# Row maxima sent by GpSimd's queue, another order of query and key parts, and an earlier residual product, in a pipelined attention graph

## The reference, cut to what matters

```python
nodes = {-1: inputs}
for c in range(6):
    nsrc = min(c + 1, 5); snode = c - nsrc
    q = ew[c, 0] * (nodes[c - 1] @ We[eq] + be[eq])
    k = ew[c, 1] * (nodes[snode] @ We[ek] + be[ek])
    v = ew[c, 2] * (nodes[snode + nsrc // 2] @ We[ev] + be[ev])
    o = _mha(q, k, v, Wq[c], Wk[c], Wv[c], Wo[c])    # softmax over 256 keys, per batch and head
    nodes[c] = act_w[c] * o + q
out = layernorm(nodes[5]) * ln_g + ln_b
x = x + out
```

## Time and profile before

| | |
|---|---|
| Median of 3 runs | 1074.8 us (1071.63 to 1077.8) |
| Profiled execution, its own time | 1070.5 us |
| Its span, first to last instruction | 1068.3 us |
| Granted TensorE clock, mean | 0.984 |
| Busy: TensorE, VectorE, ACT, POOL | 991.6, 834.6, 732.0, 450.0 us |
| DMA issues: st (SP), mst (SP), stores (POOL) | 576 of 128 KB, 192 of 6 KB, 15 of 128 KB |

### The profile page before, as it was taken

The page is one execution under the profiler, slowest core; times in us unless marked ns, Lnnn a source line. Parts: engine busy times, 40 slices in busy tenths (PEclk is TensorE's granted clock), DMA queues, the critical chain, the costliest instruction groups (busy, mean ns, idle before and its releaser), DMA issues.

```text
span 1068.3 us, 26897 instructions
## 1 busy us (share of the span) xinstructions
PE 991.6 (93%) x9705; PEld 701.8 (66%) x9705; DVE 834.6 (78%) x1791; ACT 732.0 (69%) x1605; POOL 450.0 (42%) x885
## 2 busy tenths in 40 slices
PE   8889999988899999999999999999999999999994
PEld 4755656554676677677676777676776777767763
DVE  5557777766789987888788899878887887888883
ACT  3446666663677777777777777877777777777774
POOL 3522222332343334334543458743344335434455
PEclk9989999999999999999999999999999999999997
DMA  8100000006666666666567577666766766775640
GB/s 226 35 1 1 1 0 0 0 2 88 91 94 100 101 100 94 105 102 99 99 101 103 93 103 122 115 98 105 102 96 102 101 102 94 105 102 95 101 64 30
DMA packets 84439, 87.33 MB, mean 82 GB/s; under 512 B 11610, under 2 KB 70238, under 8 KB 84318
## 3 DMA queue, kind: packets, MB, share of 16 engines
q1 hardware_dynamic: 82670, 83.56, 50.6%
q0 software_dynamic: 848, 2.11, 1.0%
q10 hardware_dynamic: 800, 0.05, 0.0%
HBM read 6.90 MB, written 2.10 MB: 8 GB/s over the span
## 4 chain that ended last, share of the span: by engine, by line
PE 45%; DMA 17%; DVE 11%; SPq 10%; ACT 6%; issue 6%; POOL 5%; DVEq 0%; ACTq 0%; POOLq 0%
PE bank L1221 44%; DMA mst<-mrows 17%; SPq L494 7%; DVE region L1136 3%; SPq L508 2%; POOL hl L582 2%; ACT region L807 2%; POOL hl L579 1%; DVE region L1068 1%; DVE region L952 1%; DVE region L1063 1%; PE bank L1557 1%; ACT region L783 1%; DVE region L1056 1%; DVE region L1017 0%
## 5 line engine op out<-in xcount | busy, mean ns | idle before, releaser
L1136 DVE TENSOR_REDUCE region<-bank 128x2 f32<-128x512 f32 x768 | 488.5, 679 | 123.9 <-PE bank L1221 117.8
L807 ACT ACTIVATE region<-bank 128x512 f32<-128x512 f32 x768 | 409.7, 610 | 59.2 <-PE bank L1221 59.1
L1221 PE MATMUL bank<-st 48*128 48x256 f32 x3072 | 325.2, 330 | 5.6 <-DVE region L1136 4.2
L1221 PEld LDWEIGHTS bank<-st 48*128 48x128 f32 x3072 | 250.8, 189 | 28.2 <-DVE region L1136 4.7
L579 POOL TENSOR_TENSOR hl<-qk,one_col 128x512 fp32r<-128x512 f32 x96 | 99.9, 1041 | 400.0 <-ACT qk L772 400.0
L1221 PE MATMUL bank<-region 128*32 128x256 f32 (+3 forms) x3554 | 247.9, 375 | 2.2 <-DVE region L1163 1.2
L1221 PEld LDWEIGHTS bank<-region 128*32 128x32 f32 (+2 forms) x3554 | 129.2, 116 | 85.0 <-issue 16.4
L1221 PE MATMUL bank<-mst,ones 64*128 64x512 bf16 x768 | 151.3, 387 | 26.1 <-DMA mst<-mrows 23.6
L582 POOL TENSOR_TENSOR hl<-qk,hl 128x512 fp32r<-128x512 f32 x96 | 122.5, 1276 | 7.5
L829 ACT ACTIVATE mrows<-bank 24x256 bf16<-24x256 bf16 x96 | 35.8, 372 | 126.7 <-PE bank L1557 126.7
L1221 PEld LDWEIGHTS bank<-mst,ones 64*128 64x128 bf16 x768 | 37.2, 93 | 90.1 <-DMA mst<-mrows 39.1
(11 more groups left out here) (190 smaller groups left out, 1273.6 us busy)
## 6 DMA issues: line engine op xcount, KB each, us to landing
st<-hl SPq DMA_DIRECT2D x576, 128.0 KB, 4.4
mst<-mrows SPq DMA_DIRECT2D x192, 6.0 KB
out<-xall POOLq DMA_DIRECT2D x15, 128.0 KB, 3.8
xall<-in_L_attn_hidden_states SPq DMA_DIRECT2D x1, 768.0 KB, 9.2
cst<-in_constants SPq DMA_DIRECT2D x1, 514.5 KB, 4.1
xT<-in_L_ffn_Wq SPq DMA_DIRECT2D x1, 384.0 KB
xT<-in_L_ffn_Wk SPq DMA_DIRECT2D x1, 384.0 KB
xT<-in_L_ffn_Wv SPq DMA_DIRECT2D x1, 384.0 KB
```

The source lines that it names most:

```text
L807: act.activation(to, x_bank(x, k, e)[:, :].rearrange("p (j q) -> p j q", j=2), ACT.Exp).then_inc(B["exp_ok"], 1)
L1136: dve.tensor_reduce(mx[s.n % 2][:, to:to + 2], s_bank(s, k, e)[:, :].rearrange("p (j k) -> p j k", j=2), AX_X, ALU.max, negate=True).then_ ...
L1221: return pe.matmul(o, w, x, start=start, stop=stop, skip_group_check=skip)
```

## The change

There are three edits.

1. `maxima_rows` becomes a function of the engine that issues it. POOL calls it behind `split_maxima(m)` and ahead of everything else of its stage. SP keeps it in the stages in which POOL has work for last nodes (`by_sync`). Each of the two buffers of mst has a semaphore for either queue.
2. The four parts lie in hl in the order K_HI, Q_LO, K_LO, Q_HI. The two splits write them there with other steps.
3. `project` is cut in two. `residual(d)` issues the residual product between `project_qk` and the third burst; `project(d)` keeps the output projection.

```diff
-K_HI, K_LO, Q_HI, Q_LO = range(4)
+K_HI, Q_LO, K_LO, Q_HI = range(4)
...
-        m_in = [sem(f"m_in{n}") for n in range(2)]
+        m_in = [[sem(f"m_in{n}{q}") for n in range(2)] for q in ("_pool", "_sync")]
...
+        def by_sync(n):
+
+            ends = [at_slot(n + M_AT, k) for k in (W_AT, V_AT)]
+            return any(e is not None and e.last for e in ends)
+
+        def rows_in(m):
+
+            same = [n for n in range(m.n % 2, m.n + 1, 2) if by_sync(n) == by_sync(m.n)]
+            return m_in[by_sync(m.n)][m.n % 2], 32 * len(same)
+
+        def maxima_rows(eng, m):
...
+            eng.wait_ge(B["mt_ok"], m.n + 1)
+            for s in range(2):
+                of = s * MROW * JH
+                eng.dma_start(mst[m.n % 2][HALF * s:HALF * s + MROW, :, :], mrows[m.n % 2][of:of + MROW * JH, :]).then_inc(rows_in(m)[0], 16)
...
             def phase(t, a, s, m, x, d, z, w, v):
-                if m is not None:
-                    maxima_rows(m)
+                if m is not None and by_sync(m.n):
+                    maxima_rows(sp, m)
                 if a is not None:
                     stack(a)
...
-                pool.tensor_tensor(to[:, 1::2, :], qk[a.n % 2], to[:, 0::2, :].bitcast(F32), ALU.subtract)\
+                pool.tensor_tensor(to[:, K_LO:Q_LO - 1:-1, :], qk[a.n % 2], to[:, K_HI::Q_HI - K_HI, :].bitcast(F32), ALU.subtract)\
                     .then_inc(B["lo_ok"], 1)
...
                 if m is not None:
                     split_maxima(m)
+                if m is not None and not by_sync(m.n):
+                    maxima_rows(pool, m)
...
                 if k == 0:
-                    pe.wait_ge(m_in[x.n % 2], 32 * x.uses(2))
+                    pe.wait_ge(*rows_in(x))
...
-            def project(d):
+            def residual(d):
+
                 to, prev = bank[OUT], source(d, GRAPH[d.c]["src"][0])
                 pe.wait_ge(B["outT_ok"].sem, B["outT_ok"].at(d.n))
                 if not d.last:
                     mm(to[:, T:2 * T], w_res[:, d.c, :], prev, stop=False)
-                    pe.wait_ge(B["ctxT_ok"].sem, B["ctxT_ok"].at(d.n))
...
                     project_qk(a)
+                if d is not None:
+                    residual(d)
                 burst((3,), (3,))
```

More of the change, by code:

```diff
@@ L451, in final_scale @@
             eng.tensor_tensor(tiles, fyn, tiles, ALU.add).then_inc(B["out_ok"], 1)
+        def by_sync(n):
[5 more added lines that the diff above has]
+        def maxima_rows(eng, m):
+            old = at_slot(m.n, 2)
+            if old is not None:
+                eng.wait_ge(B["x_ps"], old.n * UNITS + UNITS)
+            else:
+                eng.wait_ge(S["ones_ok"], 3)
+            eng.wait_ge(B["mt_ok"], m.n + 1)
+            for s in range(2):
+                of = s * MROW * JH
+                eng.dma_start(mst[m.n % 2][HALF * s:HALF * s + MROW, :, :], mrows[m.n % 2][of:of + MROW * JH, :]).then_inc(rows_in(m)[0], 16)
         block = ctx.enter_context(nc.Block())
@@ L578, in split @@
                 pool.wait_ge(B["qk_ok"], a.n + 1)
-                pool.tensor_tensor(to[:, 0::2, :], qk[a.n % 2], one_col[:, :].unsqueeze(2).to_broadcast([P, 2, T]), ALU.mult)\
+                pool.tensor_tensor(to[:, K_HI::Q_HI - K_HI, :], qk[a.n % 2], one_col[:, :].unsqueeze(2).to_broadcast([P, 2, T]), ALU.mult)\
                     .then_inc(B["hi_ok"], 1)
                 pool.wait_ge(B["hi_ok"], a.n + 1)
-                pool.tensor_tensor(to[:, 1::2, :], qk[a.n % 2], to[:, 0::2, :].bitcast(F32), ALU.subtract)\
+                pool.tensor_tensor(to[:, K_LO:Q_LO - 1:-1, :], qk[a.n % 2], to[:, K_HI::Q_HI - K_HI, :].bitcast(F32), ALU.subtract)\
                     .then_inc(B["lo_ok"], 1)
@@ L827, in copy_rows @@
                 if old is not None:
-                    act.wait_ge(m_in[old.n % 2], 32 * old.uses(2))
+                    act.wait_ge(*rows_in(old))
                 act.activation(mrows[m.n % 2][:, :], bank[IN][0:MCOLS, 0:P].bitcast(BF16), ACT.Copy).then_inc(B["mt_ok"], 1)
@@ L1582, in project @@
                     mm(to[:, T:2 * T], w_res[:, d.c, :], prev, stop=False)
-                    pe.wait_ge(B["ctxT_ok"].sem, B["ctxT_ok"].at(d.n))
+                else:
+                    for t in range(KT):
+                        mm(to[:, T + t * P:T + (t + 1) * P], prev[:, t * P:(t + 1) * P], w_res[:, d.c, :], start=(t == 0), stop=False, skip=True)
+            def project(d):
+                to = bank[OUT]
+                pe.wait_ge(B["ctxT_ok"].sem, B["ctxT_ok"].at(d.n))
+                if not d.last:
                     mm(to[:, T:2 * T], w_out[:, d.c, :], ctxT, start=False).then_inc(B["node_ps"].sem, 1)
                 else:
-                    pe.wait_ge(B["ctxT_ok"].sem, B["ctxT_ok"].at(d.n))
                     for t in range(KT):
-                        r, o = slice(t * P, (t + 1) * P), slice(T + t * P, T + (t + 1) * P)
-                        mm(to[:, o], prev[:, r], w_res[:, d.c, :], stop=False)
-                        k = mm(to[:, o], ctxT[:, r], w_out[:, d.c, :], start=False)
+                        k = mm(to[:, T + t * P:T + (t + 1) * P], ctxT[:, t * P:(t + 1) * P], w_out[:, d.c, :], start=False, skip=True)
                     k.then_inc(B["node_ps"].sem, 1)
```

## The result

The change makes the kernel slower: 1099.0 us in the median of four runs (1094.5 to 1105.4) against 1075.6, a ratio of 1.024 with an interval of 1.020 to 1.027. The prediction was 1046, and the range ended at 1077. The profiled execution has a span of 1096.8 us, against 1068.3.

The account below looks back on a forecast made before the run. TensorE was taken to bound the kernel, standing still for mst's transfer 0.34 us a stage. 76 stages x (8.13 - 7.61 - 0.15) = 28, plus 1 for leftover stages: 29 us less, 1046; range 1030 to 1077.

Parts of the forecast that it names:

- the landing of mst: Within a stage: mst's second transfer, issued by POOL, would land 7.25 us in, before TensorE wants it at 7.6.
- Rival 2: mst's data come no sooner, landing when st's backlog ends, 8.1 on average; residual product gives nothing; 1075 us; chance 0.12.
- The rule I leaned on: At the DMA engines: each goes round between queues with work, packet by packet, so mst passes st's backlog and lands at 7.25.
- rival 3: POOL's queue is slower than SP's: mst lands at 8.74, stages take 8.78, 49 us are added, 1124 us; chance 0.12.
- 8.13 - 7.79 = 0.34 a stage is the transfer: In the 76 plain stages: mean length 8.13 less TensorE's own 7.79 leaves 0.34 us of waiting for mst's transfer.
- the residual's 0.18: Third burst: moving the residual product ahead removes a 0.18 us wait for ACT's exponentials, so 7.79 a stage becomes 7.61.
- Parts in another order: st's transfers: four of six read 512 adjacent elements; costed at nothing, bounds 0.3 us a stage of earlier landing and nothing.
- the residual's 7.61 and 0.66: Signs of being right: stages of 7.61 to 7.8 us, and the third burst's eight loads within 0.66 instead of 0.84.
- POOL's split still ended by ACT: Sign of being right: POOL's next large split still waits for ACT, so what is queued behind the new wait loses nothing.
- POOL's issues of 0.55 to 0.64 us: Sign of being right: POOL's issues of mst take 0.5 to 0.8 us each, from 3.6 into the stage.
- waits of TensorE's transposition for mxp: Sign of being wrong: such a wait before the transposition of the maxima would mean POOL's loop, allowing 7.5 a stage, binds.

Follow-up runs that it names:

- the kernel with mst ahead: Kernel before plus residual and parts edits, mst kept on SP's queue but its two transfers issued ahead of the last of st's six: 1073.6 us, ratio 1.000.

## Why the prediction was wrong

**The step that failed is the landing of mst.** The prediction put the second issue at 4.10 and gave it 3.15 to land: 7.25. Measured in the changed kernel's plain stages: the second issue begins at 4.70, lands 3.55 later, at 8.24 in the median. 0.60 is the later start: POOL begins 0.65 after the rows' copy ended, where SP, when free, began 0.07 after it. 0.40 is the journey. I had taken the median store's 3.8 and subtracted for its data; the 0.4 stands on no row. Rival 2 took the 3.8 whole and came to 8.14, the nearest of my figures, by luck: its second issue was 0.36 too early and its journey 0.25 too long.

**The rule I leaned on did not help here.** The forecast needed mst to pass st's data. In the kernel with ACT's queue 274 packets of st went first. The Trainium skill, "DMA: Bandwidth & Descriptors", section "Queues, rings and completion order", has each engine go round between queues that have work; no run here shows that. Where page and measurement differ, the measurement decides. On POOL's own queue the records are less plain: mst's first packet came 1.4 us after the first issue in the changed kernel and 1.2 with a third of st left out, so it waited little; the last packet came 2.5 us after the second issue against 1.4 (medians). The page's section "Issuing engines are not separate DMA queues", by which more issuers save only issue time, was right here: the end of the data did not move forward. Counted from st's first issue, mst's last packet with data ended at 7.41 before and at 7.40 with the queue alone (means of the 58 plain stages of each kernel whose next begins with a wait for mst).

**Why it is even slower, and not the same.** Rival 2 said 1075, with stages as before; they are 8.36, between its 8.13 and rival 3's 8.78. Between st's first issue and the next stage but one the kernel with the queue alone has 8.97 instead of 8.56, 0.4 for two stages. POOL's start hardly explains it: counted in the same way, the second issue of mst begins at 5.20 before, since it stands behind st's issues in SP's list, and at 5.26 with the queue alone. Nor does the data, which end at the same time. But on POOL's queue mst's small packets go on until 7.85, where on ACT's queue they end 0.01 behind the data. The pages count the packets of POOL's queue, before and after:

```profile
q0 software_dynamic: 848, 2.11, 1.0%
...
q0 software_dynamic: 6160, 3.18, 2.0%
```

(6160 - 848) / 166 = 32 for each transfer of mst: 3 of 2 KB with the data, 13 of 16 bytes, and 16 of 4 bytes, as many as the steps by which its semaphore rises. On ACT's queue it was (3290 - 800) / 166 = 15: 12 of 512 bytes and 3 of 4. In the packet records mst's last packet ended over 0.3 us before st's last in 33 of 74 stages on SP's queue, in 36 of 71 on ACT's, but in 2 of 72 on POOL's. I read this so: with SP mst stands behind the backlog of a few engines, with POOL behind that of all 16, the slowest included. That is argued and not shown, as no run changed the number of engines alone; before, mst's small packets can't be told from st's.

**The missed loop.** "8.13 - 7.79 = 0.34 a stage is the transfer" was read inside one stage. That TensorE's own time, once mst is there, sets the stage was false: st's next transfers hang on the same stage and close a loop over two. So the residual's 0.18, exact in the burst (7.61), was swallowed: 0.7 us in 94 stages, where the sum counted 76 x 0.18 = 14. And a landing at 7.25 would not have given 7.76 either. st's own last transfer is wanted some 0.4 into the second stage (there the loads on st began to wait in the kernel with mst ahead): twice a stage + 0.4 is at least 7.69 + 8.43, a stage of 7.86 or more, an estimate. I had the rows for it: SP's issues behind six of st, full engines, and stages that alternated between 7.79 and 8.43.

**Parts in another order** were costed at nothing and gave 3.6 us (0.34%), through the loop: st's six transfers need 8.48 instead of 8.56.

**The rest of the 28.5 us of span.** 18.8 in the stages. Of these some 4.6 belong to two stages with stretches at half clock, which the kernel with the queue alone doesn't have (an estimate: they take 10.60 and 9.23, against 7.61). One stretch, in windows (length, busy us of five engines, granted clock, DMA share, GB/s):

```profile
604.00:609.00 5.00, 3.37 (x23) 2.52 (x22) 3.24 (x6) 3.81 (x9) 3.50 (x6) 1.00 0.57 76
609.00:612.00 3.00, 2.21 (x18) 1.71 (x22) 0.72 (x2) 1.08 (x2) 0.54 (x3) 0.57 1.01 146
612.00:616.00 4.00, 4.00 (x40) 2.01 (x32) 2.45 (x4) 0.37 (x1) 0.00 (x0) 0.50 0.57 65
```
```profile
609.78 0.11 PEld L1233 LDWEIGHTS bank<-mst,ones 64*128 64x128 bf16 x2 [2.61 <-DMA mst<-mrows]
```

TensorE's loads stood still for 2.61 us, the longest wait for mst; near its end, at 609.4, the clock falls to 0.50, the 1.2 GHz level, and the stage that begins there takes 10.60. The kernels with half of the steps on POOL's queue have such a stretch at waits of 2.7 and 3.1. A wait alone doesn't tell: the kernel with the queue alone has one of 1.8 and no stretch, that with ACT's queue a stretch of 3.4 us at 973.2 with no wait of the loads above 1.1. 4.8 are the end, nearly all of it POOL's drain. 5.0 are the first phase, and not the change's: the kernel with residual and parts alone has 274.6 there and that with POOL's queue in the first half 270.4. Without them 23.5 are left, the difference of the medians.

What else the prediction named held: the residual's 7.61 and 0.66, POOL's split still ended by ACT, POOL's issues of 0.55 to 0.64 us, and waits of TensorE's transposition for mxp in only 10 of 96 stages, mostly those of the last nodes.

## What to carry to other kernels

Before pricing an edit by the slack inside one stage, follow each transfer to the stage that uses it, and add up the path back to its issue. Alternating stages with a nearly constant sum of two were the mark of a loop over two here, and only what lay on that loop paid. A small transfer behind a large backlog was not freed by another queue; a smaller backlog or an earlier start of it helped (0.22 us earlier gave 8 us).

## What I had not expected of the hardware

- Transfers of SP's and ACT's queues were worked off in the order of their issues: on ACT's queue mst's first packet came 2.9 us after the issue in the median, in the stage shown behind 274 packets of SP's queue.
- POOL starts a transfer 0.65 us after the copy that it waits for ended, SP 0.07; a transfer of 6 KB on POOL's queue took 32 packets, against 15 on ACT's.
- POOL's last drain took 1.62 us with 19 transfers on its queue, and 7.0, 8.0 and 8.8 with 185, 97 and 107.
- 6.8 us at half clock began within a single wait of TensorE of 2.61 us; the second such stretch (3.4 us) came at 879.1, behind a wait of 1.8 that ended at 877.4.
